# Gated cross-attention and mixture of experts: one list a batch for each engine, keys spread by ScalarE, one shift and exp for 16 heads, down projection 512 columns wide

## The reference

```python
x = x + tanh(g_xattn) * attention(layernorm(x), ctx, ctx, mask)   # 16 heads of 16, Wq Wk Wv Wfc with biases
y = layernorm(x)
gate_logits = y @ gate_kernel                                      # 8 experts, top 2, softmax over the 2
out_e = (silu(y @ w0[e]) * (y @ w1[e])) @ wo[e]                    # 256 -> 512 -> 256
x = x + tanh(g_ffn) * sum(weight_e * out_e for the two chosen experts)
```

## Time and profile before

| | us |
|---|---|
| three runs | 1364.96, 1369.81, 1369.87 |
| median | 1369.81 |
| profiled execution | 1363.92 |
| its span, first to last instruction | 1362.3 |
| share of the span: PE, PEld, DVE, ACT, POOL | 93%, 81%, 55%, 51%, 55% |
| mean granted TensorE clock | 0.962 of full |
| first context transpose in `batch` / last | 59.9 / 592.4 |
| last instruction of routing on TensorE / first of the experts | 655.9 / 683.7 |

### The profile page before, as it was taken

How to read it: one execution, slowest core, us unless ns; L and a number is a source line. 1 busy time by engine, 2 the same in 40 slices (tenths; PEclk the granted TensorE clock), 3 DMA queues, 4 the chain that set the end, 5 groups by cost and what they waited for, 6 DMA issues and landing times.

```text
span 1362.3 us, 37316 instructions
## 1 busy us (share of the span) xinstructions
PE 1263.6 (93%) x10466; PEld 1109.6 (81%) x10467; DVE 746.4 (55%) x2524; ACT 699.2 (51%) x1780; POOL 750.6 (55%) x1197
## 2 busy tenths in 40 slices
PE   4999999999999999997099999999999999999996
PEld 3888888888888888886078888888888888888885
DVE  5788788877888878873333333333333333333332
ACT  2777677767777777774033333333333333333332
POOL 3367777776777767775434444444444444444443
PEclk9999899989999999996589999999999999999998
DMA  5034333323334333326468863333333333333332
GB/s 157 23 119 138 132 126 123 127 74 116 128 124 136 132 126 128 124 100 218 150 186 213 218 146 53 54 54 54 53 52 53 54 54 54 54 54 50 57 53 34
DMA packets 73976, 139.73 MB, mean 103 GB/s; under 512 B 11604, under 2 KB 55156, under 8 KB 71764
## 3 DMA queue, kind: packets, MB, share of 16 engines
q0 software_dynamic: 32064, 52.46, 19.7%
q1 hardware_dynamic: 39840, 86.05, 19.5%
q10 hardware_dynamic: 2036, 0.75, 0.2%
HBM read 68.95 MB, written 70.27 MB: 102 GB/s over the span
## 4 chain that ended last, share of the span: by engine, by line
PE 49%; issue 1%; DMA 0%; POOL 0%; POOLq 0%; ACT 0%
PE banks L1424 28%; PE psB L1443 14%; PE psT L1432 4%; PE psG L1409 2%; DMA out_dram<-ey,eid 0%; POOL w_part L500 0%; DMA et<-routed_rows 0%; POOL routed_rows L494 0%; POOL out_dram L551 0%; POOLq L545 0%; ACT ey L774 0%; ACT etT L756 0%; POOLq L546 0%; POOLq L306 0%; POOLq L559 0%
## 5 line engine op out<-in xcount | busy, mean ns | idle before, releaser
L1424 PE MATMUL banks<-w_all,etT 128*128 x1620 | 433.3, 403 | 0.7 <-ACT etT L756 0.7
L1424 PEld LDWEIGHTS banks<-w_all,etT 128*128 128x128 f32 x1620 | 286.3, 189 | 51.4 <-issue 3.6
L1151 DVE TENSOR_TENSOR hgT<-psT,hgT 128x512 fp32r<-128x512 f32 x135 | 93.3, 691 | 426.0 <-ACT hgT L768 426.0
L551 POOL DMA_INDIRECT out_dram<-ey,eid x135 | 216.5, 1604 | 91.4 <-issue 48.0
L546 POOL DMA_DIRECT2D et<-routed_rows x135 | 76.8, 569 | 300.6 <-issue 233.0
L1443 PEld LDWEIGHTS psB<-w_all,hgT 128*128 128x128 f32 x1620 | 208.5, 188 | 18.8 <-issue 1.3
L1443 PE MATMUL psB<-w_all,hgT 128*128 x1620 | 218.5, 284 | 0.8 <-ACT hgT L768 0.8
L774 ACT ACTIVATE ey<-psB,ewt 128x256 f32<-128x256 f32 x135 | 64.2, 475 | 234.1 <-PE psB L1443 143.8
L1279 PEld LDWEIGHTS psB<-vbd,probT 128*128 128x128 f32 x1280 | 163.1, 194 | 21.9 <-ACT probT L622 20.1
L1279 PE MATMUL psB<-vbd,probT 128*128 128x51 f32 x1280 | 168.0, 271 | 13.4 <-ACT probT L622 13.4
L762 ACT ACTIVATE hs<-banks 128x512 f32<-128x512 f32 x135 | 80.7, 598 | 185.3 <-PE psT L1432 183.4
(11 more groups left out here) (162 smaller groups left out, 2188.6 us busy)
## 6 DMA issues: line engine op xcount, KB each, us to landing
split_weights<-w_part SPq DMA_DIRECT2D x16, 1536.0 KB, 6.2
w_all<-split_weights SPq DMA_DIRECT2D x32, 768.0 KB, 4.7
et<-routed_rows POOLq DMA_DIRECT2D x135, 129.0 KB, 2.4
xb<-in_x_dram SPq DMA_DIRECT2D x32, 256.0 KB, 2.8
w_raw<-in_L_ffn_w_kernel_dram SPq DMA_DIRECT2D x32, 256.0 KB
out_dram<-x SPq DMA_DIRECT2D x64, 128.0 KB
w_raw<-in_L_ffn_wo_kernel_dram SPq DMA_DIRECT2D x16, 256.0 KB
cb<-in_ctx_dram SPq DMA_DIRECT2D x32, 77.0 KB
```

The lines of the kernel that those rows point to most:

```text
L551: gp.indirect_dma_start(out=out, out_offset=bass.IndirectOffsetOnAxis(ap=eid[:, u:u + 1], axis=0), in_=ey[:, u % 2, :], in_offset=None, co ...
L1151: dve.tensor_tensor(hgT[:, 1].rearrange("p c q -> p (c q)"), psT[:], hgT[:, 0].rearrange("p c q -> p (c q)").bitcast(F32), ALU.subtract).t ...
L1424: m = pe.matmul(banks4[:, bank], etT[:, u % 2, a, c], weight(e, c, w, n), start=(j == 0), stop=(j == len(steps) - 1))
```

## The change

Attention: each engine's `batch` becomes one list for the two tiles, in a new order. `k_split(., 0)` (cast of the keys) and `v_split(., 1)` (cast of the values' rest) go from VectorE to ScalarE as `k_high` and `v_second`; `spread_keys` goes from GpSimd to ScalarE and `mask_keys` stays on GpSimd. Maxima, subtraction and exp each handle all 16 heads in one instruction; `neg_mx`, `s_negate`, `s_neg` and `s_heads` go. Experts: `down` multiplies the high part of the hidden rows with the high and the low part of the weights side by side, into both halves of psB, and the low part with the high weights into the first half; ScalarE scales the second half into `ey`, and VectorE adds the scaled first half.

The core of the functions:

```diff
         act.copy(probT[:, c0:c1].rearrange("p c q -> p (c q)"), psT[:, 0:(c1 - c0) * P]).then_inc(t_sb, 1)
     def exp_scores(i, t):
-        act.wait_ge(s_neg, i + 1)
-        for j, h in enumerate(range(S_FULL * HB, H)):
-            act.activation(prob[:, t, h * K2:(h + 1) * K2], psS[:, S_FULL, j * K2:(j + 1) * K2], ACT.Exp,
-                           bias=neg_mx[:, t, j:j + 1], scale=scale).then_inc(s_heads, 1)
         act.wait_ge(s_sub, i + 1)
-        shifted = prob[:, t, 0:S_FULL * HB * K2]
-        act.activation(shifted, shifted, ACT.Exp, scale=scale).then_inc(p_done, 1)
+        act.activation(prob[:, t, 0:HK], prob[:, t, 0:HK], ACT.Exp, scale=scale).then_inc(p_done, 1)
     def norm_2(i, t, u4, n):
...
     def copy_row(i, u4):
         act.wait_ge(xn2_done, i + 1)
         act.copy(rows[:, u4, 1, 0:D], rows[:, u4, 0, 0:D]).then_inc(row_copy, 1)
+
+    def spread_keys(b, u):
+
+        act.wait_ge(k_sb, b + 1)
+        if known(b, 2):
+            act.wait_ge(s_ps, RG * QT * (b - 1))
+        for s in range(HP):
+            act.activation(kbd[:, u, :, :, s].rearrange("p a c k -> p (a c) k"), kT2[:].bitcast(F32).rearrange("p a c k -> p (a c) k"), ACT.Copy,
+                           scale=own2[:, s:s + 1]).then_inc(kbd_done, 1)
+
+    def k_high(b):
+
+        act.wait_ge(k_raw, DC * (b + 1))
+        if known(b, 1):
+            act.wait_ge(kbd_done, HP * b)
+        act.copy(kT2[:, 0], kT[:]).then_inc(k_hi, 1)
+
+    def v_second(b):
+        act.wait_ge(v_rest, b + 1)
+        act.copy(vparts[:, 1], vrest[:]).then_inc(v_part, 1)
     def v_first(b):
         act.wait_ge(v_nat, b + 1)
...
         act.wait_ge(ey_ps, t + 1)
         if known(t, 2):
             act.wait_ge(added, 16 * (t - 1))
-        act.activation(ey[:, u % 2], psB[:, 0:D], ACT.Copy, scale=ewt[:, u:u + 1]).then_inc(ey_done, 1)
+        act.activation(ey[:, u % 2], psB[:, D:2 * D], ACT.Copy, scale=ewt[:, u:u + 1]).then_inc(ey_low, 1)
     e_evac(0, 0)
...
             dve.scalar_tensor_tensor(out=kT[:, a], in0=psK[:, a * K2:(a + 1) * K2], scalar=bias[:, 1, a:a + 1],
                                      in1=valid[:, bass.ds(b * K2, K2)], op0=ALU.add, op1=ALU.mult).then_inc(k_raw, 1)
-    def k_split(b, part):
-        dve.wait_ge(k_raw, DC * (b + 1))
-        if part == 0:
-            dve.tensor_copy(kT2[:, 0], kT[:]).then_inc(k_hi, 1)
-        else:
-            dve.wait_ge(k_hi, b + 1)
-            dve.tensor_tensor(kT2[:, 1], kT[:], kT2[:, 0].bitcast(F32), ALU.subtract).then_inc(k_sb, 1)
+    def k_low(b):
+
+        dve.wait_ge(k_hi, b + 1)
+        dve.tensor_tensor(kT2[:, 1], kT[:], kT2[:, 0].bitcast(F32), ALU.subtract).then_inc(k_sb, 1)
     def v_split(b, part):
         if part == 0:
             dve.wait_ge(v_part, 3 * b + 1)
             dve.tensor_tensor(vrest[:], psA[0:K2, 0:D], vparts[:, 0], ALU.subtract).then_inc(v_rest, 1)
-        elif part == 1:
-            dve.wait_ge(v_rest, b + 1)
-            dve.tensor_copy(vparts[:, 1], vrest[:]).then_inc(v_part, 1)
         else:
             dve.wait_ge(v_part, 3 * b + 2)
...
-    split = S_FULL * HB
-    S_PARTS = [(psS[:, 0:S_FULL, 0:HB * K2].rearrange("p n (h k) -> p n h k", k=K2), 0, S_FULL, HB),
-               (psS[:, S_FULL:S_FULL + 1, 0:(H - split) * K2].rearrange("p n (h k) -> p n h k", k=K2), split, 1, H - split)]
-
-    def s_largest(i, t, part):
+    S_ALL = psS[:, 0:RG, 0:HB * K2].rearrange("p n (h k) -> p n h k", k=K2)
+
+    def s_largest(i, t):
         dve.wait_ge(s_ps, RG * (i + 1))
-        sv, h0, n, k = S_PARTS[part]
-        dve.tensor_reduce(mx[:, t, h0:h0 + n * k].rearrange("p (n h) -> p n h", n=n), sv, AX_X, ALU.max).then_inc(s_max, 1)
-
-    def s_negate(i, t):
-
-        dve.wait_ge(s_max, 2 * i + 1)
-        dve.tensor_scalar(neg_mx[:, t], mx[:, t, S_FULL * HB:H], -scale, None, ALU.mult).then_inc(s_neg, 1)
+        dve.tensor_reduce(mx[:, t].rearrange("p (n h) -> p n h", n=RG), S_ALL, AX_X, ALU.max).then_inc(s_max, 1)
     def s_shift(i, t):
-        dve.wait_ge(s_max, 2 * (i + 1))
-        sv, h0, n, k = S_PARTS[0]
-        dve.tensor_tensor(prob[:, t, h0 * K2:(h0 + n * k) * K2].rearrange("p (n h k) -> p n h k", n=n, k=K2), sv,
-                          mx[:, t, h0:h0 + n * k].rearrange("p (n h o) -> p n h o", n=n, o=1).to_broadcast([P, n, k, K2]),
+        dve.wait_ge(s_max, i + 1)
+        dve.tensor_tensor(prob[:, t, 0:HK].rearrange("p (n h k) -> p n h k", n=RG, k=K2), S_ALL,
+                          mx[:, t].rearrange("p (n h o) -> p n h o", n=RG, o=1).to_broadcast([P, RG, HB, K2]),
                           ALU.subtract).then_inc(s_sub, 1)
...
         dve.tensor_copy(eid[:, u:u + 1], et[:, u % 2, D:D + 1]).then_inc(eid_done, 1)
         dve.tensor_copy(ewt[:, u:u + 1], et[:, u % 2, D + 1:D + 2]).then_inc(eid_done, 1)
+    def y_sum(t, u):
+
+        dve.wait_ge(ey_low, t + 1)
+        dve.scalar_tensor_tensor(out=ey[:, u % 2], in0=psB[:, 0:D], scalar=ewt[:, u:u + 1], in1=ey[:, u % 2],
+                                 op0=ALU.mult, op1=ALU.add).then_inc(ey_done, 1)
+
     e_low(0, 0)
...
         if below(t, MOE_T - 1):
             e_low(t + 1, (u + 1) % 4)
         glu(t, u)
+        if known(t, 1):
+            y_sum(t - 1, (u - 1) % 4)
     tiles(dve, tile)
     g_low(MOE_T - 1)
+    y_sum(MOE_T - 1, (MOE_T - 1) % 4)
...
         at = ((c * 2 + part) * FR + run) * F + first
         return w_of[:, bass.ds(e, 1), at:at + n].rearrange("p o f -> p (o f)")
+    wo_of = w_all[:].rearrange("p (e c) s r f -> p e c s r f", c=DC)
+
+    def weight_pair(e, c):
+
+        return wo_of[:, bass.ds(e, 1), c // 2, :, 2, c % 2 * D:(c % 2 + 1) * D].rearrange("p o s d -> p (o s) d")
+
     def up(t, u, e, n, bank, done):
         steps = [(a, w, c) for a, w in PARTS for c in range(DC)]
         for j, (a, w, c) in enumerate(steps):
...
         pe.wait_ge(hgT_hi, t + 1)
         if known(t, 1):
             pe.wait_ge(ey_done, t)
-        steps = [(a, w, c) for a, w in PARTS for c in range(FC)]
-        for j, (a, w, c) in enumerate(steps):
-            if (a, c) == (1, 0):
-                pe.wait_ge(hgT_lo, t + 1)
-            m = pe.matmul(psB[:, 0:D], hgT[:, a, c], weight(e, c // 2, w, 2, c % 2 * D, D), start=(j == 0), stop=(j == len(steps) - 1))
+        for c in range(FC):
+            pe.matmul(psB[:, 0:2 * D], hgT[:, 0, c], weight_pair(e, c), start=(c == 0), stop=False, skip_group_check=True)
+        pe.wait_ge(hgT_lo, t + 1)
+        for c in range(FC):
+            m = pe.matmul(psB[:, 0:D], hgT[:, 1, c], weight(e, c // 2, 0, 2, c % 2 * D, D), start=False, stop=(c == FC - 1), skip_group_check=True)
         m.then_inc(ey_ps, 1)
     def expert_with_weights(t):
```

405 lines of the change are left out of this document (226 added, 179 removed).

## The result

The changed kernel takes 1290.51 us (median of 1289.27 to 1292.78, four runs), the kernel before 1367.67 on the same chip (1364.96 to 1369.87). The ratio is 0.9439, interval 0.9412 to 0.9465.

What follows compares the result with a forecast made beforehand. The prediction took a busy TensorE to bound attention and experts, with 1.6 us of stalls a batch. From the profiled 1363.9 us it took 42 (attention order) and 5 (down projection), giving 1317, range 1288 to 1350.

Steps and rivals of the forecast that it cites:

- Stalls of TensorE: Attention: TensorE's waits cost 1.6 us a batch; the new order saves 1.4, times 30 batches 42 us.
- The walk: Attention: one batch of the new order laid out by hand; TensorE without stalls, 0.3 to 0.6 us spare in four places.
- Half-clock stretches: Attention: stretches at half clock cost 3.1 us each; -12 to +6 us possible, counted as nothing.
- rival B: Attention: no gap left and the clock stays at full, 66 us off, 1298 us; chance 0.18.
- The tail: Last two batches and routing between attention and experts: nothing on their paths changes but the order, so 0 us.
- Merged chain: Attention softmax: reduction 1.40, subtraction 1.42, exp 1.25 to 1.31 us; costs nothing if it ends before the next probability transposes.
- Scaled copies 0.53: Attention: each of ScalarE's two scaled key copies of 308 elements takes 0.53 us, a pair 1.06 to 1.40.
- Loads: Attention, per batch: VectorE 14.2, ScalarE 14.1 to 14.4, GpSimd 12.3 us, all below TensorE's 17.0.
- Down projection: Experts: wide products save 50 ns a tile over 135 tiles, 6.5 us, counted as -5 after deductions.
- Added output step and the scatter chain: Experts: VectorE's addition and serial scatters (4.65 against 4.83 us a tile) stay hidden by 0.18; +0.5 us at the end.
- Rival A: Attention: the order closes only in part, a ScalarE or VectorE chain ending 0.3 to 1 us late; 1344 us, chance 0.24.
- rival C: Attention: the loop through GpSimd's scatters, made 15 us long, decides instead; 19.3 us a batch, 1377 us, chance 0.06.

Runs made afterwards that it cites:

- a_act_plus9: Changed kernel with nine unused ScalarE copies of 256 elements ahead of a batch's first exp: 1498.04 us, 1.0629 of the kernel before on the same chip.
- after_again: The changed kernel unedited, run again on a chip where the kernel before takes about 1404 us: 1357.85 us, ratio 0.9603 to the kernel before.
- a_down_narrow_again: Changed kernel with the old down projection (12 products of 256 columns, one ScalarE copy): 1360.60 us, ratio 0.9689 to the kernel before on the same chip.
- b_merged: Kernel before, old order, with one maximum, shift and exp for 16 heads: 1500.54 us, ratio 1.0676; repeated on another chip 1497.70 us, 1.0665.

## Why the prediction was right, point by point

- *Stalls of TensorE, 1.6 us a batch, of which 1.4 go.* An undisturbed batch went from 18.6 to 18.7 us to 17.04, so all 1.56 to 1.6 went. The 0.2 that I left for rounded handoffs was not needed: the spare times stayed open (exp 0.9 in both tiles against 0.6 walked; shift 1.0 against 1.1 and 1.2). 28 x 0.16 = 4.5 us. The walk itself held closely: scatters end 16.5 into the batch (walked 16.0), the next shift is ready 0.87 into it (0.8).
- *Half-clock stretches: nothing.* This term was off the most. Four lie in the 28 batches before (those take 21.75, 21.93, 20.34 and 21.94 us), none after; 28 x 1.56 = 43.7 of the 55.4 us are the stalls, 11.7 the clock. It was named as 0 to -12 and left out. The gaps were what it hung on: each of the four begins 0.1 to 0.6 us after the attends' wait of 0.47 to 0.48 us, the last of the stalls of the earlier trace rows's first tile (the other such waits, 18 of 22 from 100 to 530 us, are followed by none). TensorE has no gap at all between 100 and 500 us after, the clock stays at 2.4 GHz from 38.7 to 578.0, and a_act_plus9, which puts gaps back, has 27 such stretches in its 28 batches. With the ends of its own terms (1.6, -12 and 6 in the experts) the sum is 1298, rival B's. Leaving it out was to be made good by the median of before, which lay 5.9 above the profile: nothing of the kind came, since after the change median and profiled execution are 0.5 apart.
- *The tail: unchanged.* Wrong by 9.1 us in these two executions. By windows, TensorE's granted clock is at 1.2 GHz for 48 us there after the change (the row) and for 65 before:

```profile
578.00:626.00 48.00, 11.71 (x38) 8.72 (x39) 14.62 (x66) 6.05 (x16) 18.74 (x31) 0.50 0.53 174
```

  Before, TensorE waited 4.4 us in the last batch for ScalarE's rows, up to 626.0 us, and went on at half clock:

```profile
626.04 0.69 PE L1307 MATMUL psG<-ident,rows 128*128 128x128 f32 x2 [4.42 <-ACT rows L637]
```

  The prediction left the two last batches as they are, though the new order holds for their tiles too. How much of the 9.1 it brings stays open: on chip C the same stretch takes 93.6 us in after_again and 84.4 in a_down_narrow_again, whose lists are the same there. The wait for the first expert rows (27.7 us before by the line of L1409, 28.1 after) didn't change, as forecast.
- *Merged chain.* Reduction 1.435 (1.40 forecast), shift 1.428 (1.42), exp 1.220 (1.25 to 1.31, so ScalarE needs less than 1 ns an element). Right inside the new order; b_merged, on chips A and C, costs 6.7% with the same three instructions, so their work alone is not their price. The prediction's "costs nothing as long as its end meets the next transposes" was the right condition to put; it gave no price to an order that it doesn't fit.
- *Scaled copies 0.53.* Mean length 0.549; two end to end take 1.00 of engine time, 0.50 each. The estimate by the Trainium skill, "ScalarE: Activation LUTs", section "What ACT_TABLE_LOAD costs", of 0.54 us agrees.
- *Loads.* ScalarE 82.3 of 100 us are 14.0 a batch (14.1 to 14.4), GpSimd 12.6 (12.3), VectorE 14.9 (14.2). VectorE's excess is one instruction, the low part of the keys (L917), at 1073 ns: 311 before. It lies beside GpSimd's split of the weights:

```profile
308.95 2.58 POOL L493 TENSOR_TENSOR w_part<-w_raw,w_part 128x512 fp32r<-128x512 f32 x2
...
309.33 1.06 DVE L917 TENSOR_TENSOR kT<-kT 128x154 fp32r<-128x154 f32 x1
```

  It cost nothing, since VectorE had that time.
- *Down projection, 50 ns a tile, 5 in all.* (135 x 50 ns are 6.8 us, not 6.5.) 53 ns measured, 7.1 us, plus 2.2 from tiles that were longer than the others before (3.0 at each eighth tile, partly given back in the first ones), less 0.7 at the end (0.5 forecast; the last tile's rest went from 22.1 to 22.8 us): 8.6, against 8.4 seen. The Trainium skill's rule for a single gap, "TensorE: Matmul & The Clock Gate", section "Back-to-back issue gap", would give 10 ns a tile; on four chips the runs give 44 to 57.
- *Added output step and the scatter chain.* Hidden, as forecast. The margin of 0.18 us shows: GpSimd waits 72.9 us in 34 places for its accumulating transfer, where before it was 11.6 in 7. When these landed late (the chain has 5.90, 3.91 and 4.86 us near 633 to 645 us), one tile grew to 5.23.
- *Rival A and rival C* are out: no wait of TensorE for exp or for the shift is left on the first chip. C's loop through the scatters closes with 1.0 us to spare.

The sum as it came: -43.7 (stalls), -11.7 (clock), -9.1 (tail), -8.4 (experts) = -72.9. Forecast were -42, 0, 0, -5. The mechanism was right, all stalls of the list went; all four terms came out on the faster side, 26 us together, and the time fell inside 1288 to 1350 by 2.5 us only because that range had been opened downwards for rival B.

## What to carry to other kernels

On a busy TensorE, count a gap with the half-clock stretch that follows it: an order that closes the last gaps gained more here than their sum (55.4 for 43.7 us), and a single stop of 2 us a batch (a_act_plus9) lost more than the whole change had saved. Price a merge of instructions together with the order around it: here the same merge is part of a gain of 4 to 6% with one order and costs 6.7% with the other, the latter on chips where results of TensorE come late beside scatters. And when one stall is repaired, look which instruction stands next on the same list, since its own releaser may be as late.
